# A graph network on one core: the receivers' table of the edge blocks held as three exact bf16 parts

## The reference, cut to what matters

```python
e = _ln(_mlp(edge_feat, ...))                 # 412500 x 64
n = _ln(_mlp(node_feat, ...))                 # 12500 x 64
for s in range(2):
    ce = concatenate([e, n[senders], n[receivers]], axis=-1)
    e = e + _ln(_mlp(ce, edge_blk_w0[s], edge_blk_b0[s], edge_blk_w1[s], edge_blk_b1[s]), ...)
    agg = segment_sum(e, receivers, num_segments=12500)
    n = n + _ln(_mlp(concatenate([n, agg]), ...), ...)
```

## Time and profile before

| | |
|---|---|
| median of 3 runs | 22607.06 us |
| the profiled execution | 22640.54 us |
| its span | 22638.8 us |
| PE busy | 13646.0 us (60%) |
| PE weight loads busy | 10718.9 us (47%) |
| DVE busy | 9714.0 us (43%) |
| ACT busy | 2931.8 us (13%) |
| POOL busy | 11698.9 us (52%) |
| mean granted TensorE clock | 0.693 of full |

### The profile page before, as it was taken

One profiled execution on the slowest core, in us unless ns is written; L12 is line 12 of the kernel. 1 busy time (PEld: TensorE's weight loads), 2 busy tenths in 40 slices (PEclk: granted clock), 3 DMA queues, 4 the chain that ended last, 5 costly groups with the idle time before them and its releaser, 6 DMA issues. The chain is left out here.

```text
span 22638.8 us, 317898 instructions
## 1 busy us (share of the span) xinstructions
PE 13646.0 (60%) x88696; PEld 10718.9 (47%) x88696; DVE 9714.0 (43%) x29825; ACT 2931.8 (13%) x5120; POOL 11698.9 (52%) x12296
## 2 busy tenths in 40 slices
PE   2555555554787777845655555555456666666664
PEld 1444444443677677734444444444334444444443
DVE  4333333333666666643333333333343333333333
ACT  0222222221000000011111111111111111111111
POOL 5656565565444444444444444444445555555553
PEclk7666666565899899966666666666666666666666
DMA  2111111112111001113333333333323333333331
GB/s 86 54 55 55 55 55 54 56 54 58 20 21 21 20 20 21 21 44 102 102 101 102 102 101 102 102 102 101 88 78 93 92 93 92 93 92 93 91 92 53
DMA packets 1995040, 1603.29 MB, mean 71 GB/s; under 512 B 1291419, under 2 KB 1461007, under 8 KB 1994047
## 3 DMA queue, kind: packets, MB, share of 16 engines
q10 hardware_dynamic: 939256, 906.14, 12.2%
q0 software_dynamic: 394560, 282.16, 6.6%
q1 hardware_dynamic: 661104, 413.62, 6.5%
HBM read 990.92 MB, written 612.64 MB: 71 GB/s over the span
## 5 line engine op out<-in xcount | busy, mean ns | idle before, releaser
L804 POOL DMA_INDIRECT s_gt<-ta_d,s_ix x6448 | 6148.6, 954 | 5990.0 <-DVE s_ix L857 3804.4
L804 POOL DMA_INDIRECT g_gt<-xs_d,g_ix x3224 | 3047.6, 945 | 2084.4 <-DVE g_ix L857 1069.4
L1001 PE MATMUL pair<-g_part,g_Oh 128*128 128x224 bf16 x25389 | 2994.4, 276 | 750.9 <-issue 723.6
L1001 PEld LDWEIGHTS pair<-g_part,g_Oh 128*128 128x128 bf16 x25389 | 2531.5, 104 | 1123.4 <-issue 1001.4
L804 POOL DMA_INDIRECT g_gt<-ys_d,g_ix x2015 | 1921.1, 953 | 2124.8 <-DVE g_ix L857 1509.5
L1048 PEld LDWEIGHTS psw<-s_R,s_P 128*128 128x128 f32 x12896 | 2016.7, 228 | 2071.3 <-issue 2045.3
L1048 PE MATMUL psw<-s_R,s_P 128*128 128x64 f32 x12896 | 2001.9, 303 | 1421.6 <-issue 1392.9
L1015 PE MATMUL pair<-e_w,s_hT 128*128 128x128 f32 x6448 | 1350.9, 376 | 2240.6 <-ACT s_hT L953 1652.8
L1048 PE MATMUL psw<-g_R,g_P 128*128 128x80 f32 x6448 | 1250.3, 374 | 1831.2 <-ACT g_sg L958 1775.7
L1015 PEld LDWEIGHTS pair<-e_w,s_hT 128*128 128x128 f32 x6448 | 1195.0, 277 | 2385.4 <-ACT s_hT L953 1369.0
L1048 PEld LDWEIGHTS psw<-g_R,g_P 128*128 128x128 f32 x6448 | 1178.6, 282 | 2289.4 <-issue 2267.1
(11 more groups left out here) (329 smaller groups left out, 15662.6 us busy)
## 6 DMA issues: line engine op xcount, KB each, us to landing
s_dl<-dl_d SPq DMA_DIRECT2D x404, 512.0 KB
seg_d<-s_sg ACTq DMA_DIRECT2D x806, 256.0 KB
seg_d<-g_sg ACTq DMA_DIRECT2D x403, 320.0 KB
z_d<-g_rT ACTq DMA_DIRECT2D x403, 256.0 KB
s_z<-z_d ACTq DMA_DIRECT2D x403, 256.0 KB
s_gt<-ta_d,s_ix POOLq DMA_INDIRECT x6448
s_Bw<-tb_d ACTq DMA_DIRECT2D x3224, 32.0 KB
s_Bw<-tb_d SPq DMA_DIRECT2D x3224, 32.0 KB
```

Of the source, the lines that this page charges most:

```text
L804: eng.indirect_dma_start(out=gt[k][:, s, :], out_offset=None, in_=table[:, :], in_offset=bass.IndirectOffsetOnAxis(ap=ix[k][:, s:s + 1], a ...
L1001: last = eng.matmul(near_out(k, t), Oh[k][:, g, 128 * t:128 * t + 128], part[n][:, g, :, :].rearrange("p f l -> p (f l)"), start=g == 0 an ...
```

## The change: the parts of the receivers' table

- `tb_d` holds 192 bf16 values a row instead of 64 f32: three parts whose sum is the f32 value. A window `Bw` is 48 KB instead of 32 KB; the number of DMAs stays.
- `Pt` is bf16 instead of f32.
- Per tile there are three bf16 matmuls instead of one in f32; PE goes by pairs of tiles (h = 0, 1) for each part n.
- In `ne` and `n0` a new stage 8, on DVE, splits the right half of `AB` into `TB` (three casts and two subtractions for each group) at the end of a round, and SP's store into `tb_d` waits for it (`n_tb`).
- The three edge bias tables share one tile `e_b1s`, at partitions 0, 32 and 64, and `ones3` becomes part of `ones67`, so that the bias matmul reads both at the same partitions.
- A small DRAM tensor `none_d` takes the place of the rows of `tb_d` that `seg64_d` was blanked from.

```diff
-        tb_d = dram("tb_d", (NP + 128, 64))
+        tb_d = dram("tb_d", (NP + 128, 192), BF16)
+        none_d = dram("none_d", (128, 64))
...
-        e_b1 = [sbuf(ctx, f"e_b1_{i}", [3, 512], BF16) for i in range(3)]
-        ones3 = sbuf(ctx, "ones3", [3, 128], BF16)
+        e_b1s = sbuf(ctx, "e_b1s", [67, 512], BF16)
+        e_b1 = [e_b1s[32 * i:32 * i + 3, :] for i in range(3)]
+        ones67 = sbuf(ctx, "ones67", [67, 128], BF16)
+        ones3 = ones67[0:3, :]
...
-                    Pt, dl, Bw = many("Pt", [128, G * 128]), many("dl", [128, 2 * G * 128], BF16), many("Bw", [128, G, 64], n=4)
+                    Pt, dl = many("Pt", [128, G * 128], BF16), many("dl", [128, 2 * G * 128], BF16)
+                    Bw = many("Bw", [128, G, 192], BF16, n=4)
...
-                        eng.dma_start(Bw[k][:, first + t, :], tb_f[bass.ds(at[t], 128 * 64)].rearrange("(p f) -> p f", f=64)
+                        eng.dma_start(Bw[k][:, first + t, :], tb_f[bass.ds(at[t], 128 * 192)].rearrange("(p f) -> p f", f=192)
...
-                            eng.matmul(ps[2 + k][:, :], ones3[:, :], mlp[1][:, :], start=False, stop=True,
+                            eng.matmul(ps[2 + k][:, :], ones67[32 * mlp[1]:32 * mlp[1] + 3, :], e_b1[mlp[1]], start=False, stop=True,
...
-                                for s in range(G):
-                                    t, q, half = SLOT_TILE[s], s // 2, 64 * (s % 2)
-                                    eng.matmul(ps[k][half:half + 64, 128 * q:128 * q + 128], Bw[(b - L_PRE) % 4][:, t, :],
+                                for q, n, h in itertools.product(range(4), range(3), range(2)):
+                                    t = SLOT_TILE[2 * q + h]
+                                    eng.matmul(ps[k][64 * h:64 * h + 64, 128 * q:128 * q + 128], Bw[(b - L_PRE) % 4][:, t, 64 * n:64 * n + 64],
                                                Pt[k][:, 128 * t:128 * t + 128], start=False, stop=False, skip_group_check=True)
...
-                ORDER, BEHIND = (6, 2, 3, 4, 7, 5, 0, 1), (0, 0, 1, 1, 2, 2, 3, 3)
+                ORDER, BEHIND = (6, 2, 3, 4, 7, 5, 0, 1, 8), (0, 0, 1, 1, 2, 2, 3, 3, 3)
...
+                        eng.wait_ge(*n_tb(n + 1))
                         eng.dma_start(tb_d[0:NP, :].rearrange("(p c) f -> p c f", p=128)[:, g:g + m, :],
-                                      AB[k][:, 0:m, 64:128]).then_inc(n_ab[k].sem, 16)
+                                      TB[k][:, 0:m, :]).then_inc(n_ab[k].sem, 16)
...
+                        if s == 8 and not dec:
+                            bv, tv = AB[k][:, 0:m, 64:128], TB[k][:, 0:m, :]
+                            eng.wait_ge(*n_out(n + 1))
+                            for i in range(3):
+                                last = eng.tensor_copy(tv[:, :, 64 * i:64 * i + 64], bv)
+                                eng.drain()
+                                if i < 2:
+                                    eng.tensor_tensor(bv, bv, tv[:, :, 64 * i:64 * i + 64], ALU.subtract)
+                                    eng.drain()
+                            last.then_inc(n_tb.sem, 1)
```

More of the change, by code:

```diff
@@ L1 @@
+import itertools
 import concourse.bass as bass
@@ L238, in sp @@
                     eng.dma_start(car_d[:, NT:NTP], zrow[0:2, 0:NTP - NT]).then_inc(d_car.sem, 16)
-                    eng.dma_start(tb_d[NP:NP + 128, :], zrow[:, 0:64]).then_inc(d_kept.sem, 16)
+                    eng.dma_start(tb_d[NP:NP + 128, :], zrow[:, 0:96].bitcast(BF16)).then_inc(d_kept.sem, 16)
+                    eng.dma_start(none_d, zrow[:, 0:64]).then_inc(d_kept.sem, 16)
                     eng.wait_ge(*v_made(CN))
@@ L254, in sp @@
                     eng.dma_start(solo_d.rearrange("(o n) -> o n", o=1), chain[0:1, :]).then_inc(d_kept.sem, 16)
-                    eng.wait_ge(*d_kept(16 * 5))
+                    eng.wait_ge(*d_kept(16 * 6))
                 def act(eng):
@@ L294, in dve @@
                     eng.memset(ones[:, :], 1.0)
-                    eng.memset(ones3[:, :], 1.0)
+                    eng.memset(ones67[:, :], 1.0)
                     eng.memset(one2[:, :], 1.0)
@@ L351, in dve @@
                     eng.wait_ge(*d_ends(32))
-                    eng.tensor_scalar(basei[:, :], bn[0:1, :], 64.0, None, ALU.mult)
+                    eng.tensor_scalar(basei[:, :], bn[0:1, :], 192.0, None, ALU.mult)
                     eng.memset(same[:, 0:1], 0.0)
@@ L754, in windows @@
                     _, at = nc.values_load_multi_w_load_instructions(
-                        basei[0:1, bass.ds((j - L_BW) * G + first, 4)], engines=[which], min_val=0, max_val=N * 64,
+                        basei[0:1, bass.ds((j - L_BW) * G + first, 4)], engines=[which], min_val=0, max_val=N * 192,
                         skip_runtime_bounds_check_because="a tile's first dst is a node's number")
                     for t in range(4):
-                        eng.dma_start(Bw[k][:, first + t, :], tb_f[bass.ds(at[t], 128 * 64)].rearrange("(p f) -> p f", f=64)
+                        eng.dma_start(Bw[k][:, first + t, :], tb_f[bass.ds(at[t], 128 * 192)].rearrange("(p f) -> p f", f=192)
                                       ).then_inc(s_bw[k].sem, 16)
@@ L772, in sp @@
                     if held is not None:
-                        eng.dma_start(seg64_d[:, NT - 96:NT, :], bc(tb_d[NP:NP + 128, :].rearrange("w (o f) -> w o f", o=1), [128, 96, 64])
+                        eng.dma_start(seg64_d[:, NT - 96:NT, :], bc(none_d.rearrange("w (o f) -> w o f", o=1), [128, 96, 64])
                                       ).then_inc(s_blank.sem, 16)
@@ L1242, in norm16 @@
             return eng.tensor_tensor(x[:, :, :], x[:, :, :], b16(st[2]), ALU.mult)
-        edge_loop("g1", 16, xs_d, seg80_d, mlp=(e_w1[0], e_b1[0]), attr=True, zout=z_d, ew2=ew, counted=0)
+        edge_loop("g1", 16, xs_d, seg80_d, mlp=(e_w1[0], 0), attr=True, zout=z_d, ew2=ew, counted=0)
         def conv1():
@@ L1345, in build @@
         edge_loop("g2", 16, ys_d, seg16_d, ew2=ew, held=ys[:, :, :], xp=XP)
-        n_in, n_t, n_x, n_h, n_hid, n_mlp, n_sq, n_ss, n_rr, n_new, n_nt, n_nT, n_u, n_out, n_dec, n_fin, n_end = [
-            mark(f"n_{n}") for n in ("in", "t", "x", "h", "hid", "mlp", "sq", "ss", "rr", "new", "nt", "nT", "u", "out", "dec", "fin", "end")]
+        n_in, n_t, n_x, n_h, n_hid, n_mlp, n_sq, n_ss, n_rr, n_new, n_nt, n_nT, n_u, n_out, n_dec, n_fin, n_end, n_tb = [
+            mark(f"n_{n}") for n in ("in", "t", "x", "h", "hid", "mlp", "sq", "ss", "rr", "new", "nt", "nT", "u", "out", "dec", "fin", "end", "tb")]
         n_ab = [mark(f"n_ab{k}") for k in range(2)]
@@ L1365, in node_phase @@
                 AB = two("AB", [128, 8, 128]) if not dec else None
+                TB = [sbuf(c, f"{tag}_TB{b}", [128, 8, 192], BF16) for b in range(2)] if not dec else None
                 d2 = two("d2", [128, 512]) if dec else None
@@ L1602, in node_phase @@
                     x.passed(n_groups)
+                if not dec:
+                    n_tb.passed(n_groups)
                 n_ab[0].passed(32 * ((n_groups + 1) // 2))
@@ L1607, in build @@
         cg.close()
-        edge_loop("s0", 64, ta_d, seg64_d, mlp=(e_w1[1], e_b1[1]), expand=True, zsrc=z_d, zw=zw[0], zout=e_d, counted=1)
+        edge_loop("s0", 64, ta_d, seg64_d, mlp=(e_w1[1], 1), expand=True, zsrc=z_d, zw=zw[0], zout=e_d, counted=1)
         node_phase("n0", seg64_d, nb_w0[0], n_b0[1], 1, edges=1, nxt=1)
-        edge_loop("s1", 64, ta_d, seg64_d, mlp=(e_w1[2], e_b1[2]), expand=True, zsrc=e_d, zw=zw[1], counted=2)
+        edge_loop("s1", 64, ta_d, seg64_d, mlp=(e_w1[2], 2), expand=True, zsrc=e_d, zw=zw[1], counted=2)
         node_phase("n1", seg64_d, nb_w0[1], n_b0[2], 2, edges=2)
```

## The result

The changed kernel takes 22235.42 us (median of 4 runs, 22169.02 to 22263.24) against 22603.37 us of the kernel before in the same comparison: ratio 0.9837, interval 0.9818 to 0.9856, so 368 us less. The forecast was 22496 with a range from 22370, so the direction was right and the gain more than three times too small. Its profiled execution took 22215.21 us.

What follows compares the result with a forecast made beforehand. The prediction took the loops as bound by a chain of waits, with `Pt` between PE's held signals' release and the next gathers. Terms -127 - 32 + 35 + 13 = -111 took 22607 to 22496 us, range 22370 to 22700.

Steps and rivals of the forecast that it cites:

- The failed step: In s0 and s1, a shorter `Pt` gains 0.27 us at each of POOL's 470 waits for indices: -127 us.
- The last part: List of what the profile after would show, and which signs, such as changed gathers between POOL's waits, would be wrong.
- The held signals: In s0 and s1, PE's signals are often held back while POOL gathers; one in s1 came 4.9 us late.
- the faster rival: PE is on the path in most turns: -242 us instead of -32, 22290 us or less; chance 0.13.
- `Pt`'s duration: DVE's instruction for `Pt` in the edge loops falls from 752 ns to 483 ns with bf16 output.
- Its worth: `Pt`'s gain of 0.27 us over 470 waits, 251 in s1 and 219 in s0: -127 us.
- The product: PE's product of `Pt` and `Bw` takes 0.84 or 1.64 us by clock; 211 direct waits, half counted: -32 us.
- The slower rival: PE's instruction stream, starved during gathers, has its waits grow by half: 22677 or 22858 us; chance 0.18.
- The windows: Loads of `Bw`, 384 bytes a row instead of 256, are covered by a lead of two turns: 0 us.
- Stage 8: Five DVE instructions a group in the node phases, 3.2 us: +35 us in n0, +13 us in ne.

Runs made afterwards that it cites:

- e5: The changed kernel with `Pt` written by two instructions of 512 elements: 22487.02 us, 0.9873 of the kernel before.
- e11: The changed kernel with only the first part multiplied, 8 bf16 matmuls instead of 24: 23041.37 us, 1.0118 of the kernel before.
- e6: The kernel before with the product's f32 matmuls taking 96 of 128 moving columns: 22805.60 us, ratio 1.0021.
- e12: The kernel before with each f32 matmul of the product cut into three, 24 instead of 8: 24180.72 us, ratio 1.0606.
- e13: The changed kernel with the third part multiplied twice, 32 bf16 matmuls instead of 24: 22710.25 us, 0.9970 of the kernel before.
- c1: The changed kernel itself, unaltered, run again: 22232.40 us, 0.9836 of the kernel before.

## Why the prediction was wrong

- **The failed step** is the sentence that `Pt`'s gain "counts each time that POOL waits for the indices, 470 times", and in the other turns is worth nothing: the number of waits, and with it the share of long batches, was taken as fixed. The last part had named the danger, a changed number of gathers between two waits that "moves the turns by more than any term of the sum"; it got no price and no chance. It was worth 401 of the 500 us in s1 (e5, with `Pt` as long as before, has 5296 against 5697), the rest being `Pt`. It could have been priced from the trace: 97 turns in batches of 8 at 13.12 us stood beside 14.99 in the 16s. What showed in its place: the 24 matmuls of the product end the long batches of s1 (e11), a number that the prediction counted only as a cost.
- **The held signals** were read rightly ("often held back"), but those that are not held got a price only in the faster rival, and there as a gain. In the kernel before, 129 of the 249 first layers that were ready within 7 us of a burst's first gather got through inside it, and it is these that lengthen a batch.
- **`Pt`'s duration**: 487 ns against a forecast of 483. Right. Its worth: 99 us in s1 (e5), where all turns wait; nothing in s0, where I had 219 x 0.27 = 59.
- **The product**: 1.05 and 1.49 us against 0.84 and 1.64. The pairs overlap in bf16. Its time alone is worth 15 us in s1 and none in s0 by e6, against 32; the two profiles of e6 and of the kernel before are too few to tell 15 us from nothing. Half right.
- **The faster rival** (PE on the path in most turns, 22290) came near the number by the wrong mechanism: it had signals escape the hold more often. They escape less often, and that is the gain.
- **The slower rival**, PE's stream: the waits for issue in the product's line fell from 515 to 20 us in s1 and from 209 to 168 in s0 instead of growing by half, since a product outside a long batch is not starved. But its mechanism is real: with 78 records it costs 6% (e12), with 62 it eats most of the gain (e13). The changed kernel's 54 stand at that edge.
- **The windows** at nothing: no cost shows in s1, where a turn in a batch of 8 went from 13.12 to 12.88 us, `Pt`'s gain alone. In s0 the store of `e_d` waits behind them in ACT's queue. From the store's issue to DVE's 864 or 870 the median is 2.16 us in the kernel before and in e6, with 32 KB a tile, and 2.52, 2.50 and 2.46 in the changed kernel, c1 and e5, with 48 KB. This fits s0's 20 to 56 us more, in place of 59 less, but no run took the larger windows away on a holding chip, so the cause stays open.
- **Stage 8**: a round of 11.22 us against 11.4 forecast, n0 34 us longer against 35, ne 20 against 13 (bounds 0 to 39). Right: cast 0.43, subtraction 0.69.

## What to carry to other kernels

Where a loop's turns come in two patterns, price the change of pattern before the change of any instruction: count how often each occurs, what a turn takes in each, and what tips one into the other. An early release is no gain if it lets work start where it runs starved. And a time of one chip need not be that of the next: the same program took 22600 and 16157 us here, and the change gave 1.6% on one kind and 0.6% on the other.
